# Six PSUM banks for the weight transposes of the drain, and four DMA channels instead of eight for the transposing loads

## The reference

```python
def _quantize(w):
    gamma = jnp.mean(jnp.abs(w))
    return jnp.clip(jnp.round(w / (gamma + EPS)), -1.0, 1.0)
def _bitlinear(x, w):
    return jnp.matmul(x, _quantize(w).T)

# attention: q, k, v = x @ W.T; rope; causal softmax(q k^T / sqrt(128)) v; @ Wo.T
# ffn:
x1 = _bitlinear(x, w1); x2 = _bitlinear(x, w2)
hidden = jax.nn.sigmoid(x1) * x2
return _bitlinear(hidden, w3)

x = x + _layernorm(attn(_layernorm(x)))
x = x + _layernorm(ffn(_layernorm(x)))
```

## Time and profile before

| | us |
|---|---|
| median of 2 runs | 11379.07 |
| the two runs | 11325.12 and 11433.03 |
| the profiled execution | 11333.62 |
| its span, core 6 (the slowest; the cores span 11202.5 to 11332.0) | 11332.0 |

### The profile page before, as it was taken

The page is one execution under the profiler, slowest core; times in us unless marked ns, Lnnn a source line. Parts: engine busy times, 40 slices in busy tenths (PEclk is TensorE's granted clock), DMA queues, the critical chain, the costliest instruction groups (busy, mean ns, idle before and its releaser), DMA issues.

```text
span 11332.0 us, 111192 instructions; the slowest of 8 cores (11202.5 to 11332.0 us)
## 1 busy us (share of the span) xinstructions
PE 6812.9 (60%) x31276; PEld 3094.8 (27%) x31808; DVE 2899.6 (26%) x5841; ACT 2594.9 (23%) x5541; POOL 917.6 (8%) x1556
## 2 busy tenths in 40 slices
PE   0646662222221154998489853577745799759983
PEld 0223331111111022443144321233322343224431
DVE  1334664333333233000100013334433100010001
ACT  0243663333333222000100001116622100000001
POOL 0121113222223100000000000000000000000000
PEclk9967775555555577999799986787777899978887
DMA  6453224333322322221222122210032222121112
GB/s 110 114 157 105 71 69 161 109 108 112 111 92 94 80 75 97 75 78 57 81 94 77 58 76 71 59 39 1 1 80 78 93 77 64 60 108 63 61 54 83
DMA packets 584022, 921.29 MB, mean 81 GB/s; under 512 B 329600, under 2 KB 420224, under 8 KB 562304
## 3 DMA queue, kind: packets, MB, share of 16 engines
q0 software_dynamic: 134688, 552.70, 15.6%
q1 hardware_dynamic: 448736, 361.44, 10.8%
HBM read 715.69 MB, written 174.06 MB: 79 GB/s over the span
## 4 chain that ended last, share of the span: by engine, by line
PE 44%; DMA 16%; DVE 14%; issue 9%; SPq 8%; ACT 8%; DVEq 1%; ACTq 0%; POOL 0%; POOLq 0%
PE PS L1005 11%; PE PS L1012 11%; SPq L128 8%; PE PS L1049 7%; DMA ARENA<-w3T_h 6%; PE PS L929 4%; DMA w3T_h<-ARENA 3%; PE PS L852 3%; PE PS L497 3%; DVE ARENA L344 2%; PE PS L815 2%; DVE PS L824 2%; ACT ARENA L829 2%; DVE ARENA L370 2%; DVE ARENA L507 1%
## 5 line engine op out<-in xcount | busy, mean ns | idle before, releaser
L1005 PE MATMUL PS<-ARENA 128*128 128x512 bf16 x5518 | 1713.7, 392 | 405.1 <-DMA ARENA<-w2T_h 398.3
L1012 PE MATMUL PS<-ARENA 128*128 128x512 bf16 x5520 | 1713.9, 392 | 6.7
L1049 PE MATMUL PS<-ARENA 128*128 128x512 bf16 x5520 | 1351.8, 390 | 232.2 <-DMA ARENA<-w3T_h 174.7
L497 PE MATMUL PS<-ARENA 128*128 128x128 bf16 x2112 | 506.6, 264 | 1632.4 <-ACT ARENA L504 1307.6
L344 DVE TENSOR_REDUCE ARENA<-ARENA 128x1 f32<-128x2048 f32 (+1 forms) x128 | 292.6, 2286 | 2868.8 <-ACT ARENA L1059 1597.8
L1005 PEld LDWEIGHTS PS<-ARENA 128*128 128x128 bf16 x5632 | 564.2, 100 | 1106.4 <-issue 580.1
L1025 DVE TENSOR_TENSOR ARENA<-ARENA,PS 128x1024 bf16<-128x1024 f32 x176 | 215.0, 1222 | 2445.7 <-ACT ARENA L1021 2445.7
L829 ACT ACTIVATE ARENA<-PS 128x512 bf16<-128x512 f32 x1280 | 764.2, 597 | 283.9 <-DVE PS L824 207.1
L1049 PEld LDWEIGHTS PS<-ARENA 128*128 128x128 bf16 x5632 | 519.8, 99 | 1064.3 <-issue 621.6
L713 PE MATMUL PS<-ARENA 128*128 128x512 bf16 x2508 | 630.2, 414 | 283.0 <-DMA ARENA<-wq_bf 185.6
L1012 PEld LDWEIGHTS PS<-ARENA 128*128 128x128 bf16 x5632 | 564.6, 100 | 709.1 <-issue 182.5
(11 more groups left out here) (79 smaller groups left out, 5028.9 us busy)
## 6 DMA issues: line engine op xcount, KB each, us to landing
ARENA<-w POOLq DMA_DIRECT2D x1056, 256.0 KB, 3.8
ARENA<-w1T_h SPq DMA_DIRECT2D x176, 512.0 KB, 3.4
ARENA<-w2T_h SPq DMA_DIRECT2D x176, 512.0 KB, 3.2
ARENA<-w3T_h SPq DMA_DIRECT2D x704, 128.0 KB, 2.0
ARENA<-x POOLq DMA_DIRECT2D x64, 1024.0 KB, 6.8
y_h<-ARENA POOLq DMA_DIRECT2D x32, 1024.0 KB, 4.1
ARENA<-y_h POOLq DMA_DIRECT2D x32, 1024.0 KB, 5.2
out<-ARENA POOLq DMA_DIRECT2D x32, 1024.0 KB, 4.1
```

Of the source, the lines that this page charges most:

```text
L497: e.transpose(ps, src, ident[:]), inc="T")
L1005: e.matmul(px1[wi][:, seg * 512:(seg + 1) * 512], w1sl[:, wi, dc, :], ln2Th[:, dc, seg * 512:(seg + 1) * 512], start=(dc == 0), stop=(dc = ...
L1012: "tensor", lambda e, dc=dc, seg=seg, wi=wi: e.matmul(px2[wi][:, seg * 512:(seg + 1) * 512], w2sl[:, wi, dc, :], ln2Th[:, dc, seg * 512:(s ...
L1049: "tensor", lambda e, i=i, hc=hc, wi=wi: e.matmul(pfs[i], hidT[:, hc, i * P:(i + 1) * P], w3sl[:, wi, :], start=(hc == 0), stop=(hc == c.H ...
```

## The change

It has two parts.

First, a third set of PSUM banks. `ptq6` names banks 2 to 7, a flag `drain` is set for the time of the drain only, and `transp_item` takes the six banks in turn (`dc % 6`) while the flag is set, and the two old ones otherwise. Even blocks still go to ACT and odd ones to DVE, so ACT has banks 2, 4 and 6 and DVE 3, 5 and 7. No other stage is at work in the drain, and there is a barrier on both sides of it. All 132 items run in the drain.

Second, the channels of the transposing DMAs, in QKV and for Wo, are taken modulo 4 instead of 8. So a transposing DMA waits for the one four before it, no longer for the one eight before it, and PE waits for four channels instead of eight at the start of a group.

```diff
@@ -404,8 +404,9 @@
     pts_g = [psbf(i, 0) for i in range(2)]
     ptq_g = [psbf(2 + i, 0) for i in range(2)]
+    ptq6 = [psbf(2 + i, 0) for i in range(6)]
     pt_tok_g = [None, None]
-    ptq_tok = [None, None]
+    ptq_tok = [None, None, None, None, None, None]
@@ -487,23 +488,25 @@
         def fn():
+            nrot = 6 if pst.get("drain") else 2
+            rot = ptq6 if nrot == 6 else ptq_g
             b.wait("tensor", vtok)
             last_t = None
             for dc in range(c.DC):
-                ps = dc % 2
+                ps = dc % nrot
                 b.wait("tensor", ptq_tok[ps])
                 src = wqh[:, tpar, dc, :]
-                ttok = b.emit("tensor", lambda e, src=src, ps=ptq_g[ps]:
+                ttok = b.emit("tensor", lambda e, src=src, ps=rot[ps]:
                               e.transpose(ps, src, ident[:]), inc="T")
@@ -693,8 +696,8 @@
                     b.dma("sync", wb[:, dc, :], srcw, transpose=True,
-                          ch=f"ws{cg % 2}_{dc % 8}")
-                ws_toks = [b.dma_total(f"ws{cg % 2}_{j}") for j in range(8)]
+                          ch=f"ws{cg % 2}_{dc % 4}")
+                ws_toks = [b.dma_total(f"ws{cg % 2}_{j}") for j in range(4)]
@@ -894,17 +897,19 @@
         b.barrier()
         pst["eng_pref"] = "ALT"
+        pst["drain"] = True
         while QV:
             drip(QV, 1)
         while QT:
             QT.popleft()()
+        pst["drain"] = False
         b.barrier()
@@
             b.dma("sync", woT[:, dc, :], wo_bf[0:c.D, dc * P:(dc + 1) * P],
-                  transpose=True, ch=f"wo{dc % 8}")
-        wo_loaded = [b.dma_total(f"wo{j}") for j in range(8)]
+                  transpose=True, ch=f"wo{dc % 4}")
+        wo_loaded = [b.dma_total(f"wo{j}") for j in range(4)]
```

More of the change, by code:

```diff
@@ L502, in fn @@
                 if eng == "scalar":
-                    fn2 = (lambda e, dc=dc, ps=ptq_g[ps]:
+                    fn2 = (lambda e, dc=dc, ps=rot[ps]:
                            e.copy(slab[:, dc * P:(dc + 1) * P], ps))
                 else:
-                    fn2 = (lambda e, dc=dc, ps=ptq_g[ps]:
+                    fn2 = (lambda e, dc=dc, ps=rot[ps]:
                            e.tensor_copy(slab[:, dc * P:(dc + 1) * P], ps))
```

## The result

| us | before | changed |
|---|---|---|
| median of all executions timed with it | 11621.27 (10) | 10881.82 (12) |
| lowest and highest | 11325.12 and 11743.23 | 10799.61 and 11226.66 |
| profiled execution | 11333.62 | 10879.78 |
| its span | 11332.0 (core 6) | 10878.0 (core 7) |

Between the medians of all executions lie 739 us, and not the 439 of the forecast: executions in which some cores get a lower TensorE clock weigh on both medians, and the ratios leave them out as far as they can.

A forecast was written before the change was run, and what follows sets the result against it. No engine is full; a chain of waits bounds the drain, PE and the copying engines handing one bank back and forth. 11333.6 - 439 (454 from six banks, less 15 for four channels) = 10895 us; range 10760 to 11060.

The forecast's parts named there:

- the upper bound: Drain, six banks: at most 472 us saved, if w1, w2 and w3 slices of uneven length become regular too.
- the irregular slices: Drain: mean slices of 14.36 and 17.11 us against 14.27 and 16.85 shown; becoming regular would save 7 + 11 us more.
- the engine pace: Drain copies with six banks: ACT every 0.35 us, DVE every 0.33, seen within copy pairs; saves 297 + 157 us.
- the pace of rows 7: Rival, drain copies: 0.82 us for two, 0.41 each, as in the output projection; saves 375 us, time 10974; chance 0.12.
- The detour of the store behind DVE's first instruction: Drain, w3: POOL's store issues only when DVE's first quantizing instruction ends, at 3817.1 us, not the 3816.8 otherwise expected.
- the discount from 21 to 15: First sequence's QKV halves: four channels cost 21 us by the working, taken as 15; fewer in flight might land sooner.
- The bound of 49: QKV with four channels: largest cost, if a landing takes 6.8 us: 0.38 x 130 = 49 us.
- too few in flight: Rival, SP's waits before 768 QKV transposing DMAs: at 9 us landing four channels cost 714 us, time 11594; chance 0.01.
- the sum: Whole kernel: 454 us saved in the drain less 15 us for the four channels, 439 us.
- an execution without it would end up to 107 us sooner, one with one more such half 107 later: Feed-forward: one half at 0.81 clock on core 6 costs its two up lines 107 us; left out of the costs.
- its time is 45 us under the median of the two runs ... I stay with the sum: Starting time: the profiled 11333.6 us was kept as base, though the two runs lie 108 us apart.
- The rival of the spread clock: Rival: all four feed-forward halves run at 0.81 clock, giving back 321 us, time 11216; chance 0.06.

## Why the prediction was right or wrong

**First part: right, to 2%.** Predicted 454 us off the drain, measured 448 (2022 to 1574). w1 and w2: 10.90 us a slice predicted, 10.88 in the regular slices, 297 us predicted and measured. w3: 13.3 predicted, 13.38 in a regular slice, 157 us predicted and 150 measured (in the upper bound the 7 us for the irregular slices should be 8, which changes nothing); the irregular slices stayed as irregular as they were, 0.3 us of 13.7. The step that chose the engine pace (0.33 and 0.35 us) over the pace of rows 7 (0.41) was right, and the run with four banks shows that the other would have been right for four.

**The detour of the store behind DVE's first instruction** held: on core 7 of the changed kernel 84 of the 88 stores of w1 and w2 and 41 of the 44 first stores of w3 are released by L577, as in the row of 2861.25. (Rows 5 and 6 show it for the kernel before; rows 4, which the prediction names, do not.) In the last w3 slices ACT's fence ends the wait, with the same result within 0.1 us.

**Second part: right in place and sign, undersized.** The working gave 21 us and I took 15, half a guess that the landing shortens. With four channels it did not (above), and 21 us is what SP took longer; the quick core spans are 21 to 25 us longer. The step that failed is the discount from 21 to 15. The bound of 49 held. The neighbouring rival, too few in flight, fell: even two channels cost 100 us, nearly all of it in two halves.

**The fixed cost of a DMA.** The Trainium skill's 2.3 us for a 128 KB store ("DMA: Bandwidth & Descriptors", "Anatomy of one DMA — SWDGE (gpsimd) path") against 2.52 us from issue to issue: the trace has the issue of 0.54 us in line with the landing of 2.0, and the row was the better number. For one store of 512 KB the rule gives 3.2 us; measured are 3.5 to 3.7 for w3, and 3.2 for w1 and w2.

**The time: what was wrong is the starting point and the step from the sum to the medians.** The forecast took 11333.6, one profiled execution, for the time of the kernel before; its median came out at 11621.27, 288 us above that. The change between the medians is 739 us, where the sum has 439. That 10895 was forecast and 10881.82 measured owes much to chance: in the starting execution core 6 lost about 120 us to the low clock (its fourth feed-forward half took 1125 us, the others 1001 to 1004), and the median of the changed kernel happens to lie 82 us above its lowest execution. What the sum really foretells is the difference between undisturbed cores: 439 us, where the quick ends of the spans give 431 to 437 on one chip and the two parts on the traces 448 - 21 = 427. Two steps failed:

- "an execution without it would end up to 107 us sooner, one with one more such half 107 later". The low clock is not one half more or less. Single cores were up to 557 us over the quickest in the kernel before and up to 488 in the changed one. The up lines of core 4 above took (408 - 380) ns x 11264 = 315 us more; that is stretches in three of the four feed-forward halves.
- "its time is 45 us under the median of the two runs ... I stay with the sum". Two executions and a profiled one say little about a kernel whose executions reach from 11228 to 11743 us: in the later comparisons its median was 11293, 11493 and 11621 us. Between medians of all executions the drop was 332 us (six banks alone), 527 and 739 us for nearly the same kernel. A forecast by sums of durations can only be held against the ratio of undisturbed ones.

The rival of the spread clock was put as something that the change might bring. The table of spans shows none of it: the excess is 115.5 us before and 103.8 after. Its price of 107 us for a half is near the 120 that core 6 lost. One sign of being wrong did come, 0.81 stretches in another half: in the changed kernel's profile cores 6 and 7 had them in the third (1061 and 1072 us in place of 999 to 1008), not in the fourth. As they move about in both kernels, this says nothing against the sum. The Trainium skill's rule ("TensorE: Matmul & The Clock Gate", Part 1: with three cores of a die in dense matmuls the whole die drops to 13/16) gives the level that the rows show, 0.81, but here all eight cores run dense matmuls in every feed-forward half and most halves have 1.00; the 0.81 also came to a single pair of cores. By the rule every execution of both kernels would be disturbed, and 57 to 66% of the core spans were not.

What the low clock follows is open. It was seen in both kernels, on different chips, cores and halves; no run here made it come or stay away.

## What to carry to other kernels

Two engines that hand a buffer back and forth are paced by the round trip divided by the buffers each has, until the slower engine's own step is longer: read the round trip from a place in the same trace that already has more buffers, and the step from two instructions that follow each other without a wait. Three banks were enough here (0.82 / 3 = 0.27 under 0.33); the next gain lay elsewhere, in a shared scratch buffer that made two engines take turns (3.5 us a slice) and in four stores on one semaphore (2.7 us a slice). Fewer transfers in flight cost only where the landing is longer than spacing times channels; here that was where the loads of the sums filled the DMAs.

Before a forecast is compared with a median, find out how far that kernel's executions lie apart and whether the spread is in the work or in the clock: the spans of the single cores tell it, medians of few executions don't.

## What the runs showed of the hardware

- Pairs of cores, one die or both at 0.81 of the full clock for part of a feed-forward half, with neighbours at 1.00 in the same kind of work; single cores were up to 557 us over the lowest span of 11183.
- Transposing DMAs of 256 rows: issue spacing 1.32 us and landing 2.3 to 2.4 us when alone, whether two, four or eight may be in flight; beside the loads of the sums 5.1 to 5.9 us in the median with four or eight in flight, 4.5 to 5.1 with two.
- Four serial stores of 128 KB take 9.7 us, one of 512 KB from the same buffer to the same place 3.5 to 3.7.
- Late stores of w3 on pairs of cores (a wait of up to 5.8 us instead of 2.0), with slices of 15 to 17.5 us in place of 13.4; not explained.
